# Recurrence weights loaded a phase earlier, bias products made eight steps at a time, and sorted-unit additions moved to GpSimd

## The reference, cut to what matters

```python
for e in range(E):                                    # E = 4, hidden 1024
    h = gelu(context_c @ ew1[e] + eb1[e])
    y = h @ ew2[e] + eb2[e]
    out = out + w_be[:, e][:, None, None] * mask[e][None, :, None] * y
shared = gelu(context_c @ sw1 + sb1) @ sw2 + sb2
return out + shared
```

```python
xW = jnp.einsum('ntd,dh->nth', x, Wx) + b
def step(prev_h, xw_t):
    next_h = jnp.tanh(xw_t + prev_h @ Wh)
    return (next_h, next_h)
```

## Time and profile before

| | |
|---|---|
| median of 3 executions | 2395.03 us (2393.37 to 2396.66) |
| the profiled execution | 2392.26 us, its span 2390.5 us |
| PE busy | 2040.7 us (85% of the span), 13199 instructions |
| DVE busy | 1343.4 us (56%) |
| ACT busy | 981.5 us (41%) |
| POOL busy | 292.2 us (12%) |
| sorted units of the second layer | about 330 to 620 us |
| dense experts | 620 to 1333 us |
| recurrence | 1334 to 1437 us |

### The profile page before, as it was taken

The page is one execution under the profiler, slowest core; times in us unless marked ns, Lnnn a source line. Parts: engine busy times, 40 slices in busy tenths (PEclk is TensorE's granted clock), DMA queues, the critical chain, the costliest instruction groups (busy, mean ns, idle before and its releaser), DMA issues. The chain is left out here.

```text
span 2390.5 us, 33899 instructions
## 1 busy us (share of the span) xinstructions
PE 2040.7 (85%) x13199; PEld 1636.8 (68%) x13199; DVE 1343.4 (56%) x2533; ACT 981.5 (41%) x1942; POOL 292.2 (12%) x220
## 2 busy tenths in 40 slices
PE   6699699999899999999999893699936677785886
PEld 3499578888687888888888782498914564653554
DVE  2766456877765356464553214656455555544974
ACT  2244355565345445544554221235322354553222
POOL 1377000000000000000000002367510000000000
PEclk8899799999899999999999995799966767997988
DMA  2654113223014212112100110644272001001000
GB/s 81 224 163 108 42 40 102 91 88 106 1 50 105 36 36 67 29 36 77 18 13 1 47 41 1 224 134 117 34 190 51 2 19 36 18 18 38 0 9 27
DMA packets 111161, 150.46 MB, mean 63 GB/s; under 512 B 6856, under 2 KB 93431, under 8 KB 110616
## 3 DMA queue, kind: packets, MB, share of 16 engines
q1 hardware_dynamic: 99836, 130.14, 18.4%
q0 software_dynamic: 11168, 18.18, 3.8%
HBM read 124.08 MB, written 24.22 MB: 62 GB/s over the span
## 5 line engine op out<-in xcount | busy, mean ns | idle before, releaser
L1742 DVE TENSOR_TENSOR m_h_lo<-m_hf,m_h_hi 128x512 fp32r<-128x512 f32 x256 | 173.8, 691 | 310.9 <-ACT m_hf L1717 307.1
L1714 ACT ACTIVATE m_h_hi<-m_h_ps,m_bT 128x512 fp32r<-128x512 f32 x256 | 177.0, 691 | 366.8 <-PE m_h_ps L394 347.3
L639 POOL DMA_INDIRECT token_sums<-e_y,slot_row x56 | 184.2, 3289 | 105.5 <-DVE e_y L747 86.0
L1717 ACT ACTIVATE m_hf<-m_h_ps,m_bT 128x512 f32<-128x512 f32 x256 | 175.0, 684 | 0.0
L709 ACT ACTIVATE e_h_hi<-e_h_ps,e_b1T 128x320 fp32r<-128x320 f32 (+1 forms) x128 | 78.1, 610 | 166.4 <-PE e_h_ps L394 161.2
L770 DVE TENSOR_TENSOR e_h_lo<-e_hf,e_h_hi 128x320 fp32r<-128x320 f32 (+1 forms) x128 | 72.5, 583 | 112.0 <-ACT e_hf L712 106.0
L1424 DVE TENSOR_TENSOR c_h_lo<-c_hf,c_h_hi 128x512 fp32r<-128x512 f32 x120 | 82.5, 688 | 77.5 <-ACT c_hf L1380 76.2
L1377 ACT ACTIVATE c_h_hi<-c_h_ps,c_b 128x512 fp32r<-128x512 f32 x88 | 62.2, 707 | 109.7 <-PE c_h_ps L394 109.1
L394 PE MATMUL m_y_ps<-m_h_hi,l_w_1hi 128*128 128x512 f32 x256 | 100.4, 392 | 3.5 <-issue 3.5
L394 PE MATMUL m_y_ps<-m_h_hi,l_w_0hi 128*128 128x512 f32 x256 | 99.7, 389 | 1.4 <-ACT m_gT L1728 1.4
L394 PE MATMUL m_h_ps<-m_x_hi,l_w_0hi 128*128 128x512 f32 x256 | 100.2, 392 | 0.7 <-DVE m_x_lo L1736 0.7
(11 more groups left out here) (664 smaller groups left out, 5414.4 us busy)
## 6 DMA issues: line engine op xcount, KB each, us to landing
cT<-in_L_ffn_W_dram SPq DMA_DIRECT2D x30, 1024.0 KB
res<-in_L_cond_ew_dram SPq DMA_DIRECT2D x22, 1024.0 KB, 5.1
cT<-in_L_ffn_w_dram SPq DMA_DIRECT2D x16, 1024.0 KB, 4.9
res<-gates_rows SPq DMA_DIRECT2D x8, 1024.0 KB, 15.3
l_mod<-modulation_rows SPq DMA_DIRECT2D x16, 512.0 KB, 6.7
token_rows<-d_tok SPq DMA_DIRECT2D x2, 2112.0 KB, 10.4
token_sums<-res SPq DMA_DIRECT2D x2, 2048.0 KB, 7.6
res<-token_sums SPq DMA_DIRECT2D x8, 512.0 KB, 7.1
```

Source lines behind the costliest of these rows:

```text
L639: pool.indirect_dma_start(out=sums, out_offset=bass.IndirectOffsetOnAxis(ap=st.slot_row[0:r, e, j:j + 1], axis=0), in_=y[0:r, e % 2, j, :] ...
L1714: act.activation(hs[0][:, f, :], h_ps[:, f % HB, :], ACT.Relu, bias=bT[:, at:at + 1])
L1717: act.activation(hf[:, f % HB, :], h_ps[:, f % HB, :], ACT.Relu, bias=bT[:, at:at + 1]).then_inc(act_done, 1)
L1742: dve.tensor_tensor(hs[1][:, f, :], hf[:, f % HB, :], hs[0][:, f, :].bitcast(F32), ALU.subtract).then_inc(h_ready, 1)
```

## The change

Four edits:

1. Wx, Wh, b and the ones tile of the recurrence move from tiles of their own into the first half of res. They are loaded and set in the dense experts' phase, once the seventh expert has used its gates, while the eighth runs.
2. Bias products are made for eight steps of a bank at once, by 512 columns, and the steps of a bank then use eight column ranges in turn.
3. The eight additions of each sorted unit leave DVE for GpSimd, which loads a unit's eight places before it waits for yg. DVE waits for them before it writes yg again.
4. The tile parity of the last layer's conditioning is 64 bytes long in place of 8, which moves the tiles behind it by 32 bytes.

```diff
 @block.gpsimd                                   # l1_cond_phase
+            pool.wait_ge(columns_set, 1)
+            for u in range(NB, UNITS):
+                first = (u - NB) * SLOTS
+                columns = [pool.value_load(column[0:1, first + s:first + s + 1], min_val=0, max_val=N - S) for s in range(SLOTS)]
+                pool.wait_ge(y_free, u + 1)
+                for s in range(SLOTS):
+                    to = accT[:, :, bass.ds(columns[s], S)]
+                    pool.tensor_tensor(to, to, yg[:, :, s * S:(s + 1) * S], ALU.add).then_inc(y_added, 1)
+                    pool.wait_ge(y_added, first + s + 1)
...
                 dve.wait_ge(y_done, u + 1)       # out_weighted
+                if r >= 1:
+                    dve.wait_ge(y_added, r * SLOTS)
...
-            def out_add(u, s):
-                at = dve.value_load(column[0:1, (u - NB) * SLOTS + s:(u - NB) * SLOTS + s + 1], min_val=0, max_val=N - S)
-                to = accT[:, :, bass.ds(at, S)]
-                link(dve.tensor_tensor(to, to, yg[:, :, s * S:(s + 1) * S], ALU.add))
...
+            sp.wait_ge(mix_used, E8 - 1)         # l1_ffn_phase, SP
+            recurrence.load(sp)
...
+            pool.wait_ge(mix_used, E8 - 1)       # l1_ffn_phase, GpSimd
+            recurrence.set_bias(pool)
...
+    def set_bias(self, pool):
+        pool.memset(self.bias[:, :], 0.0).then_inc(self.bias_set, 1)
+        pool.memset(self.ones[:, :], 1.0).then_inc(self.bias_set, 1)
+
+    def load(self, sp):
+        sp.dma_start(self.wx[:, :, :], self.Wx.rearrange("(c p) n -> p c n", p=P)).then_inc(self.w_in, 16)
+        sp.dma_start(self.wh[:, :, :], self.Wh.rearrange("(c p) n -> p c n", p=P)).then_inc(self.w_in, 16)
+        sp.wait_ge(self.bias_set, 2)
+        sp.dma_start(self.bias[0:1, :], self.b.unsqueeze(0)).then_inc(self.bias_in, 16)
...
+    PER_BANK = BLK // (KC * C)                   # l2_cond_phase: 8
...
+        columns = lambda s: slice(s // 2 % PER_BANK * KC * C, (s // 2 % PER_BANK + 1) * KC * C)
...
-                for g in range(G):
-                    pe.matmul(sums[g * C:(g + 1) * C, s % 2, 0:KC * C], ones[:, :], slices(bias[:, :], g), start=True, stop=False,
-                              skip_group_check=True)
+                if s % (2 * PER_BANK) < 2:
+                    for g in range(G):
+                        pe.matmul(sums[g * C:(g + 1) * C, s % 2, :], ones[:, :], bc(slices(bias[:, :], g), 1, PER_BANK), start=True,
+                                  stop=False, skip_group_check=True)
...
-        parity = sb("parity", [P, 2])
+        parity = sb("parity", [P, 16])[:, 0:2]
```

More of the change, by code:

```diff
@@ L1532, in _ @@
             out_weighted(UNITS - 1)
-            for s in range(SLOTS):
-                out_add(UNITS - 1, s)
 class L1FfnSmall:
@@ L1553, in load, with l1_ffn_phase @@
         sp.dma_start(self.b2rows[:, :], b2.rearrange("e (c p) -> (e c) p", p=P)).then_inc(self.b2_in, 16)
-def l1_ffn_phase(nc, sem, st, srcT, accT, w1s, w2s, small, W1, W2, later):
+def l1_ffn_phase(nc, sem, st, srcT, accT, w1s, w2s, small, W1, W2, later, recurrence):
     STEPS, THRESH = 25, 1e-9
@@ L2061, in store, with __init__, l2_cond_phase @@
         sp.wait_ge(self.stored, 32)
-def l2_cond_phase(nc, sem, st, srcT, dstT, Wx, Wh, b, kept_gu, kept_dn, turned_gu, turned_dn):
+class RecurrenceWeights:
+    def __init__(self, sem, room, Wx, Wh, b):
+        self.Wx, self.Wh, self.b = Wx, Wh, b
+        n = KC * D
+        self.wx, self.wh = (room[:, i * n:(i + 1) * n].rearrange("p (c n) -> p c n", c=KC) for i in range(2))
+        self.bias, self.ones = room[:, 2 * n:2 * n + D], room[:, 2 * n + D:2 * n + D + B]
+        self.w_in, self.bias_in = sem.of_pool_dma("rw_w_in"), sem.of_pool_dma("rw_bias_in")
+        self.bias_set = sem("rw_bias_set")
+    def set_bias(self, pool):
[6 more added lines that the diff above has]
+        sp.dma_start(self.bias[0:1, :], self.b.unsqueeze(0)).then_inc(self.bias_in, 16)
+def l2_cond_phase(nc, sem, st, srcT, dstT, weights, kept_gu, kept_dn, turned_gu, turned_dn):
     G, C = 4, P // 4
+    PER_BANK = BLK // (KC * C)
     with ExitStack() as mem:
         sb = lambda name, shape: mem.enter_context(nc.sbuf_tensor("n2_" + name, shape, F32))
-        wx, wh, bias, h = sb("wx", [P, KC, D]), sb("wh", [P, KC, D]), sb("bias", [P, D]), sb("h", [P, 2, KC * C])
-        ones = sb("ones", [P, B])
+        wx, wh, bias, ones = weights.wx, weights.wh, weights.bias, weights.ones
+        h = sb("h", [P, 2, KC * C])
         sums = mem.enter_context(nc.psum_tensor("n2_sums", [P, 2, BLK], F32))
@@ L2091, in _ @@
         def _(pool):
-            pool.memset(bias[:, :], 0.0).then_inc(bias_set, 1)
-            pool.memset(ones[:, :], 1.0).then_inc(bias_set, 1)
             turning.clear(pool)
@@ L2110, in recur @@
                     for g in range(G):
-                        last = pe.matmul(sums[g * C:(g + 1) * C, s % 2, 0:KC * C],
+                        last = pe.matmul(sums[g * C:(g + 1) * C, s % 2, columns(s)],
                                          st.condT[:, k, :] if s == 0 else dst[:, k, :, s - 1], slices(wh[:, k, :], g), start=False,
@@ L2114, in recur @@
                 last.then_inc(made, 1)
-            pe.wait_ge(w_in, 32)
-            pe.wait_ge(bias_in, 16)
+            pe.wait_ge(weights.w_in, 32)
+            pe.wait_ge(weights.bias_in, 16)
             inputs(0)
@@ L2133, in _ @@
                 act.wait_ge(made, s + 1)
-                act.activation(h[:, s % 2, :], sums[:, s % 2, 0:KC * C], ACT.Tanh).then_inc(tanhed, 1)
+                act.activation(h[:, s % 2, :], sums[:, s % 2, columns(s)], ACT.Tanh).then_inc(tanhed, 1)
                 if s >= turning.FIRST_STEP:
@@ L3298, in _, with l1_phases @@
                 add(p)
-def l1_phases(nc, sem, st, a, back, shared, later):
+def l1_phases(nc, sem, st, a, back, shared, later, recurrence):
     with ExitStack() as mem:
@@ L3313, in l1_phases @@
                       a["L1_ffn_W1"][0], a["L1_ffn_W2"][0], small)
-        l1_ffn_phase(nc, sem, st, st.cT2, st.cT, w1s, w2s, small, *w("L1_ffn_", "W1", "W2"), later)
+        l1_ffn_phase(nc, sem, st, st.cT2, st.cT, w1s, w2s, small, *w("L1_ffn_", "W1", "W2"), later, recurrence)
 def adaln_ffn_4_layers(nc, a, out):
@@ L3346, in adaln_ffn_4_layers @@
         sem.layer_end()
-        l1_phases(nc, sem, st, a, SumsBack(sums, *y_out, res_in[0]), shared, [*w("L3_ffn_", "w_gate", "w_up", "w_down"), kept_gu, kept_dn])
+        recurrence = RecurrenceWeights(sem, st.res[:, 0:NT // 2, :].rearrange("p t d -> p (t d)"), *w("L2_cond_", "Wx", "Wh", "b"))
+        l1_phases(nc, sem, st, a, SumsBack(sums, *y_out, res_in[0]), shared, [*w("L3_ffn_", "w_gate", "w_up", "w_down"), kept_gu, kept_dn], recurrence)
         sem.layer_end()
-        l2_cond_phase(nc, sem, st, st.cT, st.cT2, *w("L2_cond_", "Wx", "Wh", "b"), kept_gu, kept_dn, turned_gu, turned_dn)
+        l2_cond_phase(nc, sem, st, st.cT, st.cT2, recurrence, kept_gu, kept_dn, turned_gu, turned_dn)
         l2_router_phase(nc, sem, st, st.cT2, st.cT, *w("L2_ffn_", "Wr"))
```

13 lines of the change are left out of this document (3 added, 10 removed).

## The result

The changed kernel takes 2384.37 us in the median of nine runs (2382.41 to 2389.10), the kernel before beside it 2395.17 us; the ratio is 0.995, with a 95% interval of 0.9935 to 0.9965. (Ratios and intervals come from all runs and not from the two medians, so they can differ from the medians' quotient by up to 0.0015.) It is faster by 10.8 us.

A forecast was written before the change was run, and what follows sets the result against it. PE was taken to set the pace in the sorted units, DVE's addition chain their end, latency the recurrence. Terms -2.6, 0, -4.1, +1.8, +2.9, -1.1, 0 sum to -3.1 us: 2389.2 profiled, median 2391.9, range 2385 to 2401.

The forecast's parts named there:

- End of the sorted units: Last eight additions, chained on GpSimd at 0.69 us each with register loads off the chain: -2.6 us (-3.8 to +0.1).
- Within the units: Sorted units' other 80 additions leave DVE: taken as 0 us, between -1.0 and +4.
- DVE rival: Sorted units: GpSimd's additions hold DVE up, so PE waits for x_low; total +9, 2404 us; chance 0.13.
- the rival's threshold: Sorted units: PE waits if each GpSimd addition keeps DVE out over 0.45 us; at 0.6 us, +12 us.
- Start of the recurrence: Early loads let PE begin the recurrence at about 1334.3 instead of 1338.43: -4.1 us.
- the fills: Wide bias products in the recurrence: first two cost +1.8 us, six later ones +2.9 us.
- The split of the first two fills: Recurrence's first two wide bias products: first priced at the fast clock, +0.6 us, second at the slow one, +1.2 us.
- The other steps: Recurrence's other 56 steps lose eight instructions each: 0.02 us a step, -1.1 us.
- here the rival: Recurrence: fewer products landing in PSUM beside ACT free the tanh, 0.1 us a step, -5.6; total -7.6, 2387.4 us; chance 0.16.
- The other rivals: Recurrence: wide products not side by side, +20, 2412 us, chance 0.03; no earlier start, +1.0, 2396 us, chance 0.07.

## Why the prediction was wrong

*End of the sorted units: right.* Forecast 0.69 an addition, measured 0.62; the register loads did leave the chain. The ratio of 1.96 in the Trainium skill, GPSIMD Engine Reference, section 3, would be 0.56 for an addition, an estimate, and measured are 0.45 alone, 1.6 times DVE's 0.286. Its advice against the move still has some truth at this place, where DVE with registers loaded ahead needs 3.4 to 3.75 us in place of 4.98; in the units the advice doesn't hold.

*Within the units: the step that failed most plainly.* I wrote "0.69 us at worst, five waits of 2.9 us in all" and then took 0, with a gain of 1.0 as the bound. The rows of the kernel before already said it, the first of them in the prediction itself: waits of 2.9 and 1.5 us on PEld's queue and 0.8 on PE's, on the engine that I had called the bound. They overlap in part, and the gaps between PE's starts, 2.98 us, give the price. Nothing in the argument set them aside; I let a loss that no row showed (contention) outweigh a gain that a row did.

*DVE rival: right mechanism, wrong size.* GpSimd and DVE do hold each other up (704 and 1242 ns against 452, and 1483 against 1226), as the Trainium skill, SBUF — State Buffer, section "Who interferes with whom", has it. It has the second wait for the whole of the first, and here DVE lost less than that, 0.26 us beside an addition that takes 0.45 alone. Against the rival's threshold of 0.45 us and its guess of 0.6 this was too little to make PE wait. The threshold itself was about right: with x_low 1.2 us early, each of the eight additions could have cost 0.15 us more, so PE would have waited from 0.41 on, an estimate. GpSimd stretched more than DVE, and nobody waits for it within a unit.

*Start of the recurrence, and the fills: right.* -4.0 for -4.1, +2.0 for +1.8, +3.1 for +2.9. The prices for rounds of 32-column products carried over. The split of the first two fills did not: the first cost 1.1 for 0.6, as the clock fell within it, and the second 0.9 for 1.2, so there the sum owes something to luck.

*The other steps: wrong, and here the rival was right.* I took 0.02 us a step, "since the density of products while ACT reads stays the same". Measured are 5.0 / 56 = 0.09, close to the rival's 0.1. The rival's reason was also wrong, though: not fewer products beside ACT, but an earlier end of the Wx products. I had written that "the products with Wx will end 0.25 us earlier" (it was 0.1, as bias products start 15 ns apart and not 31) and then let that count for nothing. The 223 ns of the tanh under wide fills and the run without Wx speak for this end as the point.

*Net.* Two terms were short by about 3 and 4 us. For both the prediction had a figure, 2.9 us of waits and 225 against 376 ns of tanh, and each was priced at next to nothing beside it.

*The other rivals* fell as expected: the fills' products did run side by side, and the recurrence did start earlier.

## What to carry to other kernels

If an engine is called the bound, every idle gap in it is a term: add them up from the starts of its instructions and price them, before contention that no row shows. In a chain of latencies, look at what the neighbour does from the start to the end of the slow link, and move the work that is in no hurry behind that which ends last; here the order alone brought the tanh as low as the wide products did (253 against 249 ns). And see to the link with the register loads: out of the chain they were worth 5.0 us on DVE, and the choice between DVE and GpSimd for what is left 1.6, but the engine that loads them must have the time: with all 88 additions DVE hadn't and lost 1.4, rid of the other units' 80 it had.

## What was not expected of the hardware

A tanh of 128x64 out of PSUM takes 223 ns, and 250 to 440 in the median when products of 32 output columns by 64 are issued beside it, with operands read from cT in steps, while 512-column products don't touch it, nor do bias products of which the last starts some 160 ns ahead of it (223 ns). In the medians it ends 38 to 105 ns behind the start of the last of them. Whether that lies in PSUM or in the reading of SBUF was not tried; the bank written doesn't decide (338 ns with a bank of its own).

In four of the nine profiled executions with the additions on DVE the granted clock fell to 0.50 once more, for about 7 us after 312 us, where PE makes the shared expert's products, and in none of the eleven with the additions on GpSimd. One with it, the kernel with wide bias products alone, and then the same window of the kernel before:

```profile
312.30:319.00 6.70, 6.01 (x14) 4.76 (x15) 1.79 (x4) 0.00 (x0) 0.00 (x0) 0.50 0.53 173
```

```profile
312.30:319.00 6.70, 6.68 (x29) 5.52 (x30) 1.22 (x1) 0.00 (x0) 0.00 (x0) 1.00 0.64 208
```

14 matmuls instead of 29 in the same 6.7 us. The stretch from the first sorted-phase product to yg is 341.0 to 342.1 us without that fall, 344.7 to 345.1 with it (346.5 where the register loads hold DVE up), and 337.8 to 338.8 with the additions on GpSimd. The 1 us within the first and the last of these goes with how long the clock stood at 0.50 between 269 and 279 us, as in the two windows above; the fall itself costs some 3 us. Coming in four of nine executions, it makes some 1.3 us on average, an estimate, of the 4.5 between the median and the terms for the additions alone. Why it should hang on the change, whose first addition comes at 396 us, stays open; four in nine may be chance.
